# A DLRM tower's last rounds: layer 2 of round 29 moved to another PSUM bank, and the PSUM halves of round 30 one unit apart

## What is computed

```
def _cin(x, Ws, bs):                       # x: [1024, 39, 16]
    h = x
    for i, (W, b) in enumerate(zip(Ws, bs)):          # three layers, L = 128
        z = einsum('bfd,bgd->bfgd', x, h)             # products of fields
        cur = relu(einsum('bfgd,fgl->bld', z, W) + b)
        h, direct = (cur[:, :64], cur[:, 64:]) if i < 2 else (None, cur)
        outs.append(direct)
    return concatenate(outs, axis=1).sum(-1)          # [1024, 256]
h = concatenate([cin, dense_ctx], axis=1)             # [1024, 272]
h = maximum(h @ W_top1 + b_top1, 0.0)                 # 512
h = maximum(h @ W_top2 + b_top2, 0.0)                 # 256
y = h @ W_top3                                        # [1024, 1]
```

## Time and profile before

| | us |
|---|---|
| median of 3 runs | 1288.57 (1287.99 to 1289.71) |
| profiled execution | 1284.82 |
| its span, first to last instruction | 1282.8 |
| PE busy | 1213.8 (95%) |
| DVE busy | 1113.0 (87%) |
| POOL busy | 1037.6 (81%) |
| ACT busy | 816.2 (64%) |

### The profile page before, as it was taken

The page is one execution under the profiler, slowest core; times in us unless marked ns, Lnnn a source line. Parts: engine busy times, 40 slices in busy tenths (PEclk is TensorE's granted clock), DMA queues, the critical chain, the costliest instruction groups (busy, mean ns, idle before and its releaser), DMA issues.

```text
span 1282.8 us, 14379 instructions
## 1 busy us (share of the span) xinstructions
PE 1213.8 (95%) x4180; PEld 768.0 (60%) x4180; DVE 1113.0 (87%) x1274; ACT 816.2 (64%) x1115; POOL 1037.6 (81%) x629
## 2 busy tenths in 40 slices
PE   0588999999999999999999999999999999999979
PEld 0344666666666666666666666666666666676645
DVE  2199999999999999999999999999999989999843
ACT  1146666666667666766666666766666778877643
POOL 7578888888888888888888888888888778888813
PEclk9999999999999999999999999999999999999989
DMA  9194455665444556655455556665545556553000
GB/s 185 31 245 102 96 129 143 147 146 138 114 116 117 120 132 147 146 147 131 107 120 119 122 139 146 147 146 120 117 117 118 120 141 145 144 144 109 16 1 1
DMA packets 102510, 156.17 MB, mean 122 GB/s; under 512 B 20811, under 2 KB 32988, under 8 KB 102322
## 3 DMA queue, kind: packets, MB, share of 16 engines
q1 hardware_dynamic: 92256, 152.56, 49.5%
q0 software_dynamic: 10176, 2.70, 2.1%
HBM read 151.31 MB, written 6.19 MB: 123 GB/s over the span
## 4 chain that ended last, share of the span: by engine, by line
PE 81%; DVE 7%; issue 4%; POOL 4%; ACT 4%; DMA 0%; DVEq 0%; ACTq 0%
PE curM L980 37%; PE curM L1005 13%; PE curM L997 13%; PE curM L998 13%; DVE z L611 4%; POOL emb L341 3%; ACT h L843 2%; PE xk L969 2%; DVE zl L689 1%; DVE zl L698 1%; ACT zh L809 1%; DVE curY L677 1%; PE h L1097 0%; PE h L1105 0%; PE curY L980 0%
## 5 line engine op out<-in xcount | busy, mean ns | idle before, releaser
L352 POOL TENSOR_TENSOR zl<-z,zh 128x1024 fp32r<-128x1024 f32 (+1 forms) x301 | 718.4, 2397 | 149.9 <-ACT zh L809 138.5
L611 DVE TENSOR_TENSOR z<-xr,h 128x1024 f32<-128x1024 f32 x456 | 548.5, 1212 | 3.6 <-ACT h L843 2.9
L980 PE MATMUL curM<-z,wf 128*128 128x512 f32 (+3 forms) x1228 | 540.7, 600 | 0.9 <-ACT h L843 0.8
L809 ACT ACTIVATE zh<-z 128x1024 fp32r<-128x1024 f32 (+1 forms) x320 | 337.8, 1057 | 290.0 <-DVE z L611 236.5
L997 PE MATMUL curM<-zh,wl 128*128 128x512 f32 (+1 forms) x828 | 380.7, 460 | 5.4 <-ACT zh L809 3.2
L341 POOL DMA_INDIRECT emb<-in_tbl_dram,idx x312 | 312.6, 1002 | 84.2 <-issue 52.1
L980 PEld LDWEIGHTS curM<-z,wf 128*128 128x128 f32 (+3 forms) x1228 | 216.1, 188 | 238.9 <-issue 216.3
L998 PE MATMUL curM<-zh,wh 128*128 128x512 f32 (+1 forms) x828 | 326.5, 394 | 0.0
L1005 PE MATMUL curM<-zl,wh 128*128 128x512 f32 (+1 forms) x828 | 260.4, 396 | 14.4 <-DVE zl L689 6.9
L843 ACT ACTIVATE h<-curM,bias 64x512 f32<-64x512 f32 x372 | 240.4, 646 | 20.0 <-DVE z L611 10.0
L689 DVE TENSOR_TENSOR zl<-curY,zh 128x512 fp32r<-128x512 f32 x240 | 164.8, 687 | 66.7 <-ACT zh L794 65.9
(11 more groups left out here) (125 smaller groups left out, 359.7 us busy)
## 6 DMA issues: line engine op xcount, KB each, us to landing
xr<-xT SPq DMA_DIRECT2D x384, 192.0 KB, 6.1
xs<-xT SPq DMA_DIRECT2D x279, 156.0 KB
xq<-xT SPq DMA_DIRECT2D x64, 256.0 KB, 7.1
emb<-in_tbl_dram,idx POOLq DMA_INDIRECT x312, 4.5
xs<-xT SPq DMA_DIRECT2D x62, 78.0 KB
xT<-xc SPq DMA_DIRECT2D x31, 78.0 KB
xr<-in_L_rec_W_dram SPq DMA_DIRECT2D x16, 144.0 KB, 6.8
xT<-xc SPq DMA_DIRECT2D x31, 40.0 KB
```

The costliest lines, as they stand in the source:

```text
L352: nc.gpsimd.tensor_tensor(zl[0:n, SNUM[r, u] % NL, :], z[0:n, z_slot(r, u), :], zh[0:n, SNUM[r, u] % NH, :], ALU.subtract).then_inc(lo_poo ...
L611: return nc.vector.tensor_tensor(z[:, slot, :].rearrange("p (a n) -> p a n", a=2), x, h, ALU.mult)
L809: nc.scalar.activation(zh[0:n, SNUM[r, u] % NH, :], z[0:n, z_slot(r, u), :], ACT.Copy).then_inc(hi_ready, 1)
L980: mm = nc.tensor.matmul(cur[:, :], wf[rows, full_at(u), a, :], z[rows, z_slot(r, u), a * N:(a + 1) * N], start=start and i == 0, stop=stop ...
```

## The change

`bank(29, 2)` is now `xk`. PE therefore waits for other counts in three places: (29,10) waits for the last reader of `xk` (the product (28,23) and the copy `xc_copied`) and no longer for `read0`; (30,0) waits for `read0` of all tiles (seven relus of round 29) and no longer for `read2`; the top waits for `read2` of round 29 besides, since it writes `xk`.

`HALF` becomes `half_lag(r)`: 1 in round 30, 2 elsewhere. In round 30, `subtract_half(u, 0)` and `product_half(u, 1)` now stand before the product of unit u+1, and `subtract_half(u, 1)` before that of u+2. ACT's `hi_half(u, 1)` stands before the conversion of u+1.

```diff
-HALF = 2
-def behind(r, u, n):
-    ru = ORDER[NUM[r, u] - n] if NUM[r, u] >= n else None
-    return ru if ru in HALVES else None
+def half_lag(r):
+    return 1 if r == STEPS - 2 else 2
+def behind(r, u, halves):
+    for n in (1, 2):
+        at = NUM[r, u] - n * halves
+        if at >= 0 and ORDER[at] in HALVES and half_lag(ORDER[at][0]) == n:
+            return ORDER[at]
+    return None
...
-            return curM[(r + (layer - 1) % 3) % 2]
+            return xk[:, :] if (r, layer) == (STEPS - 3, 2) else curM[(r + (layer - 1) % 3) % 2]
...
-                            if kind(r, u) == "P" and u + HALF > A_END + 3 * k + 3:
+                            if kind(r, u) == "P" and u + half_lag(r) > A_END + 3 * k + 3:
...
-                    second, finished = behind(r, u, HALF), behind(r, u, 2 * HALF)
+                    second, finished = behind(r, u, 1), behind(r, u, 2)
...
-                second = behind(r, u, HALF)
+                second = behind(r, u, 1)
...
-                        if u == 0 and r >= 1:
+                        if u == 0 and 1 <= r <= STEPS - 3:
                             pe.wait_ge(read2, r)
+                        if u == 0 and r == STEPS - 2:
+                            pe.wait_ge(read0, 7 * STEPS)
...
-                        if u == A_END and 1 <= r <= STEPS - 3:
+                        if u == A_END and 1 <= r < STEPS - 3:
                             pe.wait_ge(read0, 7 * (r + 3))
+                        if u == A_END and r == STEPS - 3:
+                            pe.wait_ge(z_ready, NUM[r - 1, UNITS - 1] + 1)
+                            pe.wait_ge(xc_copied, STEPS)
...
             pe.wait_ge(top_loaded, 16 * 6)
+            pe.wait_ge(read2, STEPS - 2)
             pe.wait_ge(read0, 7 * STEPS)
```

## The result

| | median, us | runs | ratio to before (95% interval) |
|---|---|---|---|
| before | 1288.87 | 20 | |
| changed | 1286.73 | 20 | 0.9984 (0.9977 to 0.9990) |

The change is 2.1 us faster (1.3 to 3.0). The forecast was 2.25 us, 1286.3. One run of each kernel was far longer (1309.78 and 3199.49 us), and the ratio leaves these two out.

What follows compares the result with a forecast made beforehand. DVE's program was taken to set round 30's pace, with the top waiting for take1. Gain 8.3 less price 5.15 is 3.15 us, less 0.9 for the clock is 2.25: 1288.57 - 2.25 = 1286.3 us, range 1284.1 to 1288.8.

Steps and rivals of the forecast that it cites:

- Edit 1: Layer 2 of round 29 put into another bank, removing PE's wait for read2 at (30,0): worth 0, at most 0.1 us.
- The gain of 8.3 us: End of round 30: (30,17)'s last subtraction leaves the wait for take1, so the top starts 8.3 us earlier.
- The price of 5.15 us: DVE in round 30: 1.13 us at units 1, 6, 17, 1.16 at unit 12, 0.60 for the last subtraction of 17.
- The disputed wait: DVE's new wait for ACT at the subtractions of (30,6), (30,12) and (30,17): 1.16 us each.
- POOL and PE are not late: End of round 30: POOL finishes (30,19) at 1227.1, PE's last matmuls at 1227.6, 1.3 us before take1.
- The clock, 0.9 us between bounds 0 and 1.75: At the top's start PE's clock may fall to half for 3.5 us, costing 1.75; the middle, 0.9 us, was taken.
- The Trainium skill's rule: PE before the top: many short pauses can swing the clock; by it the full 1.75 us is paid, gain 1.4.
- The one that ends slower: Rival: PE stays at half clock from round 30's last units into the top and becomes the bound; 1290.7 us, chance 0.06.
- rival 1: At the top's start the clock is low every time; gain 1.4 us, 1287.2 us, chance 0.20.
- PE as the bound: Rival: PE bounds round 30, so the bank edit gives up to 2.15 us on top; 1284.2 us, chance 0.05.
- The bounds of DVE's waits, 0.70 and 1.76: Rivals on DVE's round 30 waits: lower bound, gain 4.5 us, chance 0.10; upper, gain 1.3 less 0.9, chance 0.09.
- The level, 1288.57: Median us of the whole kernel before, 3.75 above its profiled time, from which the gain was subtracted.

Runs made afterwards that it cites:

- e1_bank: The bank edit alone (layer 2 of round 29 into xk) on the kernel before: 1283.75 against 1283.99 us, ratio 1.0001.
- e2_lag: The half edit alone (halves one unit apart in round 30) on the kernel before, bank as before: 1281.01 against 1283.99 us, ratio 0.9978.
- e8_lag29: The changed kernel with halves one unit apart in round 29 too: 1291.55 us against 1289.47 for the kernel before, ratio 1.0017.
- e3_move: The kernel before with only the last subtraction of (30,17) moved directly behind the product (30,19): 1275.77 against 1283.99 us, ratio 0.9935.
- e4_after: The changed kernel once more, unaltered, timed and profiled: 1280.46 us against 1283.99 for the kernel before, ratio 0.9979.
- e9_look: The changed kernel unaltered, first of three more profiled executions: clock full behind the top's start, 50.7 us from there to the end.
- e10_look: The changed kernel unaltered, second of three more profiled executions: clock fell behind the top's start, 52.4 us from there to the end.
- e11_look: The changed kernel unaltered, third of three more profiled executions: clock fell behind the top's start, 52.4 us from there to the end.
- e5_only17: The changed kernel with halves one unit apart in round 30 at unit 17 alone: 1283.90 us against 1289.47 for the kernel before, ratio 0.9961.

## Why the prediction was right

Step by step, in its order:

- **What bounds round 30.** Right. The chain is DVE's program, then `take1` on ACT, then the top. e1_bank, e2_lag and e8_lag29 each show it.
- **Edit 1 is worth 0.** Right, and for the reason given: the first four matmuls of (30,0) come 1 us earlier against the restart, and the two behind them start where they did, 1.99 us from it.
- **The gain of 8.3 us.** Right: e3_move isolates it at 8.2 us.
- **The price of 5.15 us.** Right: from the restart to the end of the last product it is 31.23 us against 26.07, 5.16 more. The disputed wait was to be 1.16 us: the subtraction of (30,6) starts 1.76 us behind the start of its half product (1205.14 and 1203.38) where 0.60 would do. The rows could give this number because the wait, though it was filled, was already there: in the earlier trace rows the subtraction followed the product before it directly, and the earlier trace rows showed that ACT had been ready only 0.10 us earlier.
- **POOL and PE are not late.** Right: POOL ends (30,19) 35.5 us from the restart (1227.07 + 4.75 = 1231.82), 35.3 were worked out; PE's last pair ends 1 us before the top.
- **The clock, 0.9 us between bounds 0 and 1.75.** Right in that the clock can fall at the top's start, and in the price of 1.7 us; by five executions the mean is 0.7. That the middle of two outcomes came so near to it is partly luck. The earlier trace rows could not decide it: the clock held there, but in e4_after and e9_look it fell behind the same pause (1.85 and 1.84 us; granted clock 0.54 in the 3.5 us behind it). And the kernel before had a nearer row that I did not read: behind the pause of 2.15 us its clock was low from 1193.0 to 1196.5. What I had wrong is the pauses of PE before the top: I gave some 1.5, 1.0 and 1.3 us, and they are 0.31, 0.69 and 0.93. I had left out that PE's first four matmuls of the next unit run in them.
- **The Trainium skill's rule** ("TensorE: Matmul & The Clock Gate", "A second HAM failure mode: psum-queue depth-cycling") had many short pauses bring the clock down without a long one. The traces of e10_look and e11_look agree that the clock can fall without a long pause, with pauses of under 1 us before the top; but it happened in two executions of five, not in each, and e5_only17 shows the fall behind a single short pause, so many are not needed.
- **The rivals.** The one that ends slower needed the clock to be low for more than 6.3 us behind the top's start; it was low for 3.4 us at most. The low clock in every execution (rival 1) held in two of five. PE as the bound fell with e1_bank. The bounds of DVE's waits, 0.70 and 1.76, weren't reached.
- **The level, 1288.57.** The median that the gain was taken from came out at 1288.87, so the gain is what counts. The 3.75 us by which it lay above the profiled execution are likely a difference between chips, which is of that size (last section).

What the prediction did not ask is whether the gain needed the price. All its numbers were on the table: 8.3 us for one subtraction of 0.60 us that stood behind a wait, 5.15 us for drawing four units together so that it comes earlier. The subtraction could be moved by itself.

## What to carry to other kernels

When one instruction stands behind a wait that it does not need, move that instruction, and not the rule that placed it: a changed distance for a whole round is paid at every unit of the round. An instruction that seems to follow its predecessor without a gap may be hiding a wait of the same length; before taking the cover away, compare its start with the end of what it really waits for. And before two traces are compared, lay them over each other at a point inside the changed stage, since here the first 110 us alone differed by more than the effect. A row of one trace that shows the clock holding behind a pause doesn't show that it will hold there the next time.

## What the runs showed of the hardware

The same kernel, with a stage that is the same to 0.01 us (37.21 or 37.22 in five executions), starts its top at full clock in three executions and sees the clock fall just behind it, 1.3 and 1.6 us after, in two. The fall costs 1.7 us, almost as much as the change brings. In all the traces with a short pause ahead of the top it came only where the clock had been low for 6.8 us in a row early in round 30.

I had not expected the stage itself to repeat so exactly. Of the 5 us between the chips most lie in the first 110 us. PE's pause of 1.78 us, at 105.38 in the trace of before, comes at 103.5 to 104.8 us in the profiled executions on two chips (e1_bank to e4_after, and e9_look to e11_look) and at 108.9 to 109.6 us on the third (e5_only17 to e8_lag29).
